# First large attention of a four-layer kernel: queries, keys and values projected as token rows and normalised along the free axis

## What is computed

```python
def _rmsnorm(x, w):
    xf = x.astype(jnp.float32)
    var = jnp.mean(xf * xf, axis=-1, keepdims=True)
    return (xf * jax.lax.rsqrt(var + EPS)).astype(x.dtype) * w
...
# layer 1, for every batch: Q = norm(x) Wq, K = ctx Wk, V = ctx Wv, split into heads of 128
# Q and K go through _rmsnorm per token and head; scores = Q K^T / sqrt(128) + mask
# softmax along the keys, times V, heads joined, times Wo, added to x
```

## Time and profile before

| what | us |
|---|---|
| three runs | 1788.86, 1790.83, 1794.28 |
| median | 1790.83 |
| the profiled execution, its own time | 1788.83 |
| span of the profile, first to last instruction | 1787.0 |
| PE busy | 1642.3 (92% of the span) |
| DVE busy | 1172.7 (66%) |
| POOL busy | 1053.3 (59%) |
| ACT busy | 811.2 (45%) |

### The profile page before, as it was taken

How to read it: one execution, slowest core, us unless ns; L and a number is a source line. 1 busy time by engine, 2 the same in 40 slices (tenths; PEclk the granted TensorE clock), 3 DMA queues, 4 the chain that set the end, 5 groups by cost and what they waited for, 6 DMA issues and landing times. The chain is left out here.

```text
span 1787.0 us, 26495 instructions
## 1 busy us (share of the span) xinstructions
PE 1642.3 (92%) x8578; PEld 1366.5 (76%) x8578; DVE 1172.7 (66%) x2367; ACT 811.2 (45%) x2584; POOL 1053.3 (59%) x1090
## 2 busy tenths in 40 slices
PE   6499974899999999999999999999999999996896
PEld 5377852688888888887888788888888888885684
DVE  4277757477777777666778765565755556555684
ACT  4297822344444444443444444444544444443442
POOL 6544411466666778665667676555766676653362
PEclk9699986999999999999999999999999999999895
DMA  6532100222222222212112231222222322220100
GB/s 214 148 67 45 43 1 11 66 65 66 65 60 60 72 73 77 55 57 60 53 54 69 69 95 60 62 63 59 75 74 82 84 78 80 80 66 8 59 25 24
DMA packets 73705, 117.22 MB, mean 66 GB/s; under 512 B 9633, under 2 KB 21281, under 8 KB 73569
## 3 DMA queue, kind: packets, MB, share of 16 engines
q1 hardware_dynamic: 73344, 115.26, 22.6%
q10 hardware_dynamic: 224, 0.26, 0.1%
HBM read 108.15 MB, written 7.34 MB: 65 GB/s over the span
## 5 line engine op out<-in xcount | busy, mean ns | idle before, releaser
L1156 POOL TENSOR_TENSOR a_probs<-a_probs,a_total 128x512 f32<-128x512 f32 x128 | 135.3, 1057 | 210.1 <-DVE a_total L1580 208.9
L62 POOL TENSOR_TENSOR a_w_lo<-k_ring,a_w_hi 128x512 fp32r<-128x512 f32 x186 | 240.5, 1293 | 14.9
L47 PE MATMUL ps<-a_wo_hi,a_oT_lo 128*128 128x512 f32 x512 | 211.9, 414 | 5.5 <-DVE a_oT_lo L62 3.9
L47 PE MATMUL ps<-k_xT_hi,a_w_lo 128*128 128x512 f32 x512 | 204.7, 400 | 5.6 <-DVE a_w_lo L62 5.6
L49 PE MATMUL ps<-k_xT_hi,a_w_hi 128*128 128x512 f32 x512 | 203.8, 398 | 0.0
L48 PE MATMUL ps<-k_xT_lo,a_w_hi 128*128 128x512 f32 x512 | 203.7, 398 | 0.0
L49 PE MATMUL ps<-a_wo_hi,a_oT_hi 128*128 128x512 f32 x512 | 201.1, 393 | 0.0
L48 PE MATMUL ps<-a_wo_lo,a_oT_hi 128*128 128x512 f32 x512 | 199.6, 390 | 0.0
L1417 ACT ACTIVATE a_v_hi<-ps 128x128 fp32r<-128x128 f32 x128 | 35.5, 278 | 359.2 <-PE ps L1265 359.2
L62 POOL TENSOR_TENSOR a_wo_lo<-k_ring,a_wo_hi 128x512 fp32r<-128x512 f32 x128 | 165.5, 1293 | 10.2
L1555 DVE TENSOR_TENSOR a_cross<-ps,a_cross 128x512 f32<-128x512 f32 x128 | 88.1, 688 | 120.0 <-ACT a_cross L1403 117.5
(11 more groups left out here) (398 smaller groups left out, 4598.0 us busy)
## 6 DMA issues: line engine op xcount, KB each, us to landing
k_ring<-in_L_wq SPq DMA_DIRECT2D x132, 256.0 KB, 2.6
k_ring<-in_L_wo SPq DMA_DIRECT2D x128, 256.0 KB, 2.6
k_ring<-in_L_wkv SPq DMA_DIRECT2D x66, 256.0 KB, 2.6
h_q_stack<-q_part SPq DMA_DIRECT2D x24, 256.0 KB, 4.3
k_ring<-in_L_main SPq DMA_DIRECT2D x12, 256.0 KB, 3.1
p_c_raw<-in_cT SPq DMA_DIRECT2D x4, 512.0 KB, 5.6
x<-in_x SPq DMA_DIRECT2D x8, 256.0 KB, 7.8
q_part<-p_part_hi SPq DMA_DIRECT2D x8, 256.0 KB, 2.6
```

Source lines behind the costliest of these rows:

```text
L47: pe.matmul(out, lhs_lo, rhs_hi, start=start, stop=False)
L62: return eng.tensor_tensor(out_lo, value, hi.bitcast(F32), ALU.subtract)
L1156: pool.tensor_tensor(heads(probs[:, :]), heads(probs[:, :]), along_last(total[:, :], S), ALU.mult).then_inc(s["probs"], 1)
```

## The change

Layer 1 works in token rows. `project_rows(m)` (PE) projects one item, m = t+3: the context tokens of the item's batch are the stationary operand, and the group's values and keys side by side the moving one (4 x 3 matmuls of 256 columns into the columns 256 to 511 of PSUM bank 0); then the four query heads (4 x 3 matmuls of 512 columns into bank 1). The values then stand as they are used and are split at once (`round_values`, `low_values`). ACT squares the 640 columns of key and queries in one instruction (`square_rows`), DVE sums them along the free axis and adds the epsilon (`sum_squares`), POOL takes the power for all five heads in one instruction (`row_scales`), DVE multiplies (`scale_rows`), and PE turns the five heads (`turn_heads`, four into the bank of the probabilities, the key into columns 0 to 127 of bank 0). ACT and DVE split the results (`round_keys`, `round_queries`, `low_keys`, `low_queries`), the key with its weight. The mask is added to the scores in one DVE instruction with their cross part (`mask_scores`), and the copy `take_cross` falls away in layer 1. `sums`, `query_scales`, `key_scales`, `scale_keys`, `spread_key_scales` and the transposes of the values go from layer 1.

The look-ahead of layer 1 is three items, and that of layer 2 six as before; `projects_of_step` projects two P a step in steps 61 to 63. The order of the chunks follows (two chunks of values and keys together, one for each pair of k tiles, and four of queries a unit, now cut by k tile instead of by head). The first six chunks, split by ACT and DVE, are now the four query chunks of unit 0 and then its two of values and keys. The second half of the feed-forward part begins at step 64.

```diff
@@ chunks_of_step, steps of layer 1
+    if r == 0:
+        before, after = [("K", v + 1, 1), ("O", v, 2)], [("O", v, 3)]
+    elif r == 1:
+        before, after = [("Q", v + 2, 0), ("Q", v + 2, 1)], []
+    elif r == 2:
+        before, after = [("Q", v + 2, 2), ("Q", v + 2, 3)], []
+    else:
+        before, after = [("K", v + 2, 0), ("O", v + 1, 0), ("O", v + 1, 1)], []
@@ class Stream
-        self.chunks = [c for T in range(-LOOK - 1, ITEMS) for part in chunks_of_step(T) for c in part]
+        self.chunks = [("Q", 0, k) for k in range(KT)] + [("K", 0, k) for k in range(2)]
+        self.chunks += [c for T in range(START, ITEMS) for part in chunks_of_step(T) for c in part]
@@ PE
+            def project_rows(m):
+
+                u, j = m // UNIT, m % UNIT
+                rows_x = [tuple(head(x, j) for x in pair) for pair in tokens(R_[half_of(u)])]
+                rows_c = [tuple(head(x, j) for x in pair) for pair in context_tokens(half_of(u))]
+                wait_from_one(pe, s["normed"], m)
+                wait_from_one(pe, s["kT_lo"], m)
+                for k in range(KT):
+                    if j == 0 and k % 2 == 0:
+                        chunk_ready(pe, ("K", u, k // 2))
+                    both = tuple(head(x, k % 2, VK) for x in home(("K", u, k // 2)))
+                    last = matmul_split(pe, bank_vk, rows_c[k], both, k == 0, k == KT - 1)
+                last.then_inc(s["vk_mm"], 1)
+                for k in range(KT):
+                    if j == 0:
+                        chunk_ready(pe, ("Q", u, k))
+                    last = matmul_split(pe, bank_q, rows_x[k], home(("Q", u, k)), k == 0, k == KT - 1)
+                last.then_inc(s["q_mm"], 1)
+
+            def turn_heads(m):
+
+                pe.wait_ge(s["normed"], m + 1)
+                wait_from_one(pe, s["pT_lo"], m - 1)
+                pe.wait_ge(s["v_lo"], m + 1)
+                for h in range(HQ):
+                    pe.transpose(head(bank_pT, h), head(rows, 1 + h), C.ident[:, :])
+                pe.transpose(bank_kT, head(rows, 0), C.ident[:, :]).then_inc(s["turned"], 1)
...
-            for t in range(-LOOK, ITEMS + 1):
-                P = t + LOOK
+            for t in range(START, ITEMS + 1):
                 if is_item(t + 1):
                     scores(t + 1)
                 if is_item(t):
                     turn(t)
                 if is_item(t - 1):
                     project_out(t - 1)
-                if 0 <= P - 1 < LAYER_ITEMS:
-                    sums(P - 1, t + 1)
-                if is_item(t + 1):
+                if is_item(t + 1) and not normed(t + 1):
                     values(t + 1)
                 if is_item(t):
                     mix(t)
-                if is_item(P):
+                if is_row(t + 2):
+                    turn_heads(t + 2)
+                if is_row(t + 3):
+                    project_rows(t + 3)
+                for P in projects_of_step(t):
                     project(P)
@@ ACT
+                if is_row(t + 2):
+                    round_keys(t + 2)
+                    round_queries(t + 2)
+                if is_item(t + 1) and normed(t + 1):
+                    exps(t + 1)
                 if is_item(t):
                     split_oT(t)
+                if is_row(t + 3):
+                    round_values(t + 3)
+                    square_rows(t + 3)
@@ POOL
+                if is_row(T + 2):
+                    row_scales(T + 2)
@@ DVE
+            def sum_squares(m):
+
+                dve.wait_ge(s["squares"], m + 1)
+                dve.tensor_reduce(scales[:, :], by_head(rows[:, :]), AX.X, ALU.add).then_inc(s["square_sum"], 1)
+                dve.wait_ge(s["square_sum"], m + 1)
+                dve.tensor_scalar(scales[:, :], scales[:, :], HD * QK_EPS, None, ALU.add).then_inc(s["veps"], 1)
+
+            def scale_rows(m):
+
+                dve.wait_ge(s["scale"], m + 1)
+                dve.wait_ge(s["v_lo"], m + 1)
+                dve.tensor_tensor(by_head(rows[:, :]), by_head(bank_rows), along_last(scales[:, :], HD), ALU.mult).then_inc(s["normed"], 1)
+
+            def low_keys(m):
+                dve.wait_ge(s["kT_hi"], m + 1)
+                hi, lo = (k_item[m % 2][:, blk(n, S)] for n in (0, 1))
+                dve.scalar_tensor_tensor(lo, bank_kT, weight[:, 0:1], hi.bitcast(F32), ALU.mult, ALU.subtract).then_inc(s["kT_lo"], 1)
```

More of the change, by code:

```diff
@@ L902 @@
 HALF_ITEMS = LAYER_ITEMS // 2
-LOOK = 6
-N_W, N_O, N_RAW = 3, 6, 3
+LOOK, ROW_LOOK = 6, 3
+START = -ROW_LOOK
+N_O, N_RAW = 6, 3
+W_PLACES, QUERY_PLACES = 5, (0, 1, 4)
 FIRST = 6
+VK = 2 * HD
+HEADS = 1 + HQ
 SIDE1 = ER + E
@@ L925, in half_of, with projects_of_step @@
     return u % LAYER_UNITS // GROUPS
+def projects_of_step(T):
+    first = LAYER_ITEMS
+    early = {first - 3: (0, 1), first - 2: (2, 3), first - 1: (4, 5), first: (6,), first + 1: (7,)}
+    if T in early:
+        return [first + n for n in early[T]]
+    return [T + LOOK] if first + 1 < T < ITEMS - LOOK else []
 def chunks_of_step(T):
     v, r = divmod(T, 4)
+    last = LAYER_UNITS - 1
+    if r == 0:
[6 more added lines that the diff above has]
+        before, after = [("K", v + 2, 0), ("O", v + 1, 0), ("O", v + 1, 1)], []
+    rows_first = [[c for c in part if 0 <= c[1] < (UNITS if c[0] == "O" else LAYER_UNITS)] for part in (before, after)]
     if r == 0:
@@ L939, in chunks_of_step @@
         before, after = [("Q", v + 2, 2), ("O", v + 1, 0)], [("O", v + 1, 1)]
[L940 to L948, removed]
+    columns_first = [[c for c in part if 0 <= c[1] < UNITS] for part in (before, after)]
+    first, second = last + 1, last + 2
+    between = {
+        57: ([("K", first, 0)], []), 58: ([("Q", first, 0)], [("Q", first, 1)]),
+        59: ([("O", last, 0)], [("O", last, 1)]), 60: ([("O", last, 2)], [("O", last, 3)]),
+        61: ([], [("Q", first, 2), ("Q", first, 3)]), 62: ([("V", first, 0)], [("K", second, 0), ("Q", second, 0)]),
+        63: ([("Q", second, 1), ("O", first, 0)], [("O", first, 1)]), 64: ([("Q", second, 2), ("O", first, 2)], [("O", first, 3)]),
+        65: ([("Q", second, 3), ("V", second, 0)], [("K", second + 1, 0)])}
+    before, after = between[T] if T in between else rows_first if T < LAYER_ITEMS else columns_first
+    before, after = list(before), list(after)
+    extra = {21: [("S", 0, 0)], 22: [("U", 0, 0)], 29: [("M", 0, 0), ("M", 0, 1)], 30: [("M", 0, 2)], 31: [("M", 0, 3)],
+             61: [("M", 1, 0)], 62: [("M", 1, 1)], 63: [("M", 1, 2)], 64: [("M", 1, 3)]}
+    after += extra.get(T, [])
     if T in (97, 99, 101, 103):
@@ L1023, in two_attentions @@
         neg_max, total = ph.sb("neg_max", HQ), ph.sb("total", HQ)
-        kn, squares, k_squares = ph.sb("kn", UNIT * S), ph.sb("squares", UNIT * S), ph.sb("k_squares", UNIT * S)
-        k_scale, k_diagonal = ph.sb("k_scale", UNIT), k_squares
-        q_scale = [ph.sb(f"q_scale{p}", HQ * UNIT) for p in (0, 1)]
+        rows, scales = ph.sb("rows", HEADS * HD), ph.sb("scales", HEADS)
         xf, rows_T = ph.sb("xf", D), ph.split("rows_T", D)
@@ L1246, in scores @@
                 wait_from_one(pe, s["sum"], t)
-                k_both = head(kT[u % 2], j, 2 * S)
-                for h in range(HQ):
-                    q_hi, q_lo = (head(x, h * UNIT + j) for x in qT[u % 2])
+                for h, (q_hi, q_lo) in enumerate(q_both):
                     out = head(bank_s, h, 2 * S)
@@ L1455, in _ @@
             act.wait_ge(stream.columns, 16 * len(stream.small))
-            for t in range(-LOOK, ITEMS + 1):
-                P = t + LOOK
-                if t < 0:
-                    for n in {-6: (0, 1), -5: (2,), -4: (3,), -3: (4, 5)}.get(t, ()):
+            for t in range(START, ITEMS + 1):
+                if t == START:
+                    for n in range(FIRST):
                         split_first(n)
-                if is_item(t + 1):
+                if is_item(t + 1) and not normed(t + 1):
                     take_cross(t + 1)
```

344 lines of the change are left out of this document (163 added, 181 removed).

## The result

| kernel | runs | median us | range |
|---|---|---|---|
| before | 4 | 1792.55 | 1788.86 to 1799.53 |
| changed | 4 | 1814.71 | 1812.12 to 1815.08 |

What follows compares the result with a forecast made beforehand. PE's instructions were taken to bound layer 1. Start to 355.9, 60 steps of 10.65, feed-forward 22 + 8 and the layer's end put item 64 11.5 us later: 1788.8 + 11.5 = 1800.3, stated as 1801; range 1783 to 1822.

Steps and rivals of the forecast that it cites:

- What bounds it; PE's work after: Layer 1 lasts as long as PE's instructions; PE's work per item falls by 0.70 us, from 10.34 to 9.64.
- The wait that is added: Layer 1, values' and keys' projection: PE waits for the turned key's low part, 0.97 us in each of 63 steps.
- The saved PE work and the new stall cancel: Layer 1's ordinary steps: 10.65 us each after against 10.68 before, -2 us over 60 steps.
- DVE in time by 0.2: Layer 1's steps: DVE is free at 5.72 us, the turned key is rounded at about 5.90, so DVE is just in time.
- Rival (c): DVE is late in every layer 1 step, 0.4 us more before the key, 24 us in all: 1825; chance 0.09.
- Feed-forward steps: 25 steps of layer 1: PE's part is 22 us in both kernels; DVE's delays add 8, bounds 0 and 15.
- The start: Layer 1's beginning: first matmul near 317.3 us, three steps waiting for their own normalisation, 3.2 for the clock; step 1 at 355.9.
- The end of layer 1: Steps 61 to 63 have two projections each: 13.8, 14.8 and 13.2 us; item 64 is turned at 1068.0, before at 1056.5.
- From there both kernels are alike: After the turning of item 64 both kernels take the same time, so the difference stays +11.5 us.
- (a): The start and the feed-forward steps cost nothing net, 8 and 3 us off the sum: 1791, no change; chance 0.25.
- (b): The key's hand-over through ACT and DVE is cheaper, 0.75 us instead of 1.00, 16 us less: 1785; chance 0.17.
- (d): Five transposes and 1 us of rest let PE's clock fall, 1.7 us a step: 1900; chance 0.04.

Runs made afterwards that it cites:

- the low part first: The changed kernel with DVE's low part of the turned key moved ahead of the feed-forward instructions and the output's addition; 1804.34 us, 1.0047 of before.
- the repetition: The changed kernel run once more without any edit, for a second profile; 1815.26 us, 1.0133 of the kernel before.

## Why the prediction was off, point by point

The place of the new wait, its releaser and its number were right; terms of the sum were mis-sized. Over the 60 steps up to item 61, and then by stretch:

| term | forecast | measured | makes |
|---|---|---|---|
| hand-over of the key, each step | 0.97 | 1.14 | +10.2 |
| PE's work with its slack, each step | 9.68 | 9.55 | -7.8 |
| feed-forward part, PE's and DVE's | 22 + 8 | 23.2 + 10.4 | +3.6 |
| start, to item 1 | 357.2 | 360.7 | +3.5 |
| steps 61 to 63 | 41.8 | 42.0 | +0.2 |
| behind item 64 | as before | 4.6 longer | +4.6 |

These make 14.3, and but for rounding the 14.1 above. The largest error is the hand-over, and it was for the most part hidden by the work that was too dear.

- **What bounds it; PE's work after.** Right in kind. The work was 9.64 + 0.04 and measured 9.55, too dear by 0.13 a step. The mixing was said to stay at 0.78 and takes 0.69 (606.97 to 607.66): the values' transpose no longer stands ahead of its first matmul. Scores and output projection take 0.02 and 0.03 more, the projection of values and keys 0.02 less than 1.54, and there is no slack of 0.04. Two readings were off without moving the sum: the five transposes are 0.47 together, so 0.095 each and not 0.11, and the earlier trace rows leave PE idle for 0.21 us a step, not 0.34.
- **The wait that is added.** Right in place, releaser and number of steps: 63, released by `a_kT`. The step that failed is the term "0.97 in each of 63 steps": the runs show 1.14. Two parts of it were too small. "The key has a scale operand on both engines, which I put at 0.04 together": the rows have 0.14, ACT 0.37 instead of 0.28 and DVE 0.34 instead of 0.29 (that the operand is the reason is likely, but not tested). And "about 0.05 back to PE" is 0.15. From the last transpose that is 1.21 instead of 1.00. The trace of the kernel before had the 0.15 where PE waits, as here, only for DVE to be done with a bank, its end at 249.90 by the first row:

```profile
249.21 0.69 DVE L824 TENSOR_TENSOR x<-x,ps 128x512 f32<-128x512 f32 x1 [1.84 <-PE ps L49]
...
250.04 0.47 PE L47 MATMUL ps<-h_wo_hi,a_oT_lo 128*128 128x512 f32 x1 [0.87 <-DVE x L824]
```

  The 0.05 stands in most rows where the first matmul behind the wait reads what DVE wrote. Why the two differ no run tests.
- **"The saved PE work and the new stall cancel."** Right in number, -0.01 a step against -0.03, but by luck: the errors of +0.17 and -0.13 cancel as well.
- **DVE in time by 0.2.** Right in the steady steps in that DVE isn't late, but the margin of 0.2 isn't there: by the rows none is left. Rival (c) was refuted there by the low part first, which left those steps unchanged.
- **Feed-forward steps.** DVE's term was +8 and is 10.4, by the run with the low part first. PE's own part was taken as equal in both, 22: after, it is 311.8 - 27 x 10.69 = 23.2, before 309.2 - 27 x 10.70 = 20.3. With the 0.04 a step of the two points above it makes the 4.6 over the forecast.
- **The start.** The first matmul came at 315.75, 1.5 earlier than forecast, and item 1 3.5 later. "3.2 in all for a clock that falls in these waits" failed: behind the first of the waits for scaled rows some 36 slots of 256 columns at 0.21 instead of 0.12 and 13 of 512 at 0.42 instead of 0.23 cost about 5.7. The wait of 1.73 for the turned probabilities of item 0 had no term. Both together less the 1.5 are 2.7 of the 3.5.
- **The end of layer 1.** 42.0 for the steps 61 to 63, forecast 41.8.
- **"From there both kernels are alike."** Alike in instructions, not in time: 4.6 us longer in this trace, 2.2 in the repetition (147.2 behind item 127), and other kernels with the same instructions lie on either side. The term was put at nothing. Of the 4.2 us behind item 127, 2.4 are gone in the repetition together with the lower granted clock; the other 1.8, at the clock of the kernel before, aren't explained. Why the clock is granted differently is open too: none of the runs moves it by itself.
- **The other rivals.** (a) fell with the start and the feed-forward steps, which do cost. (b) fell: the hand-over is dearer, not cheaper (its floor was misread too: the smallest DVE instruction in that trace takes 0.09, not 0.15). (d) fell: the granted clock is 1.00 between 370 and 660 with five transposes a step, and with nine; between 700 and 990 the changed kernel has 0.99, as the kernel before has. The Trainium skill (TensorE: Matmul & The Clock Gate, PE-mode transpose) says that a transpose doesn't count as busy in the same way as a matmul, and that the full clock doesn't engage for it; in these stretches the trace shows no loss from them.

The failure is thus one of sizes: the hand-over, the start and the feed-forward terms were each too small, the last layer had no term, and only the work was too dear, which made up for most of the hand-over. What is left, 14.1, is more than the forecast itself. The wait exists because the key's transpose and the projection write one bank that ACT and DVE still read. The Trainium skill (PSUM — Partial Sum Buffer, PSUM bank collisions raise a hardware error) asks for exactly such a guard by bank; no run here shows what happens without it.

## What to carry to other kernels

When a result must pass through ACT and DVE before PE may write its bank again, look for PE work that goes to another bank and put it in between: here the order of two loops is worth 79 us, more than three times what the whole change cost. Price a hand-over by the forms with the operands that it really has, and its way back to the waiting engine by a wait of the same kind (here 0.15, not 0.05), and write down each term of a sum whose parts cancel, since the sum can be right by luck and the next edit then isn't. A first step that waits for its own result can pay twice, as here: once for the wait and once for the slower clock behind it.

## What the runs showed of the hardware

- A PE to ACT to DVE to PE hand-over of one 128x128 tile takes 1.21 us from the start of the last transpose, 1.14 net of the step, though the tile itself is small.
- POOL's power takes 1.17 us for five columns (below), against 1.01 for four:

```profile
L1216 POOL TENSOR_TENSOR a_scales<-a_scales,neg_half 128x5 f32<-128x5 f32 x64 | 74.8, 1169 | 176.1 <-DVE a_scales L1584 176.0
```

- The same DVE instruction (`a_xf<-x`, 128x512) takes 0.54 in most rows and 1.51 to 1.60 at 722.7, 762.2 and 800.2 of the changed kernel and 1.53 at 1146.1 of the kernel before: in these four it starts within 0.05 us of one of POOL's subtractions of 128x512 and ends 0.27 to 0.28 behind it. Beside POOL's power of a few columns it stays at 0.54.
- After rests of 3 to 4 us PE was at the lower of its two levels for most of the matmuls that followed the key's hand-over, and once, at 350.8, after one of 1.73. Rests of 0.94 in every step left it at the upper one from item 1 to 30 (1.00 between 370 and 660).
